# First attention of a two-layer transformer block: its prologue in another order

## The reference

```python
x = x + tanh(g_xattn[0]) * L0_xattn(layernorm(x), ctx, ctx, Wq, bq, Wk, bk, Wv, bv, Wo, bo)   # 16 heads of 16
x = x + tanh(g_ffn[0])   * L0_ffn(layernorm(x), ...)        # slot routing, top 8 of 64
x = x + tanh(g_xattn[1]) * L1_xattn(ctx, layernorm(x), ...) # 8 heads of 128
x = x + tanh(g_ffn[1])   * L1_ffn(layernorm(x), ...)        # quantized gated FFN

def L0_xattn(Q, K, V, ...):
    q, k, v = Q @ Wq + bq, K @ Wk + bk, V @ Wv + bv
    scores  = einsum('bhqd,bhkd->bhqk', q, k) / sqrt(16)
    return einsum('bhqk,bhkd->bhqd', softmax(scores), v) @ Wo + bo
```

## Time and profile before

| | us |
|---|---|
| three runs | 1004.11, 998.09, 996.44 |
| median | 998.09 |
| the profiled execution, its own time | 998.65 |
| its span in the profile | 996.9 |
| PE, DVE, ACT, POOL busy | 843.5, 720.1, 507.2, 73.2 |

### The profile page before, as it was taken

One profiled execution on the slowest core, in us unless ns is written; L12 is line 12 of the kernel. 1 busy time (PEld: TensorE's weight loads), 2 busy tenths in 40 slices (PEclk: granted clock), 3 DMA queues, 4 the chain that ended last, 5 costly groups with the idle time before them and its releaser, 6 DMA issues. The chain is left out here.

```text
span 996.9 us, 16711 instructions
## 1 busy us (share of the span) xinstructions
PE 843.5 (85%) x5560; PEld 675.4 (68%) x5563; DVE 720.1 (72%) x1646; ACT 507.2 (51%) x1056; POOL 73.2 (7%) x135
## 2 busy tenths in 40 slices
PE   3359999996557659999999989999899999995657
PEld 3247777764334547888888868888688888884223
DVE  6337788774558548888888768788688887775777
ACT  2036666663314125655556546556455565553665
POOL 1000101000130000000000000000000000000241
PEclk9669999999768769999999989999999999998797
DMA  3362222201300040000000000000000000000002
GB/s 103 106 195 81 85 85 85 75 19 30 152 0 1 1 116 12 2 0 12 1 11 2 1 14 2 1 12 1 4 12 1 1 1 1 1 1 18 13 0 85
DMA packets 37518, 33.41 MB, mean 34 GB/s; under 512 B 9586, under 2 KB 36276, under 8 KB 37172
## 3 DMA queue, kind: packets, MB, share of 16 engines
q1 hardware_dynamic: 37428, 32.28, 10.1%
...
## 5 line engine op out<-in xcount | busy, mean ns | idle before, releaser
L1367 ACT ACTIVATE c_probs<-c_pS,c_neg_max 128x512 f32<-128x512 f32 x128 | 88.2, 689 | 120.2 <-DVE c_neg_max L1489 120.1
L1489 DVE TENSOR_REDUCE c_neg_max<-c_pS 128x1 f32<-128x512 f32 x128 | 88.3, 690 | 70.6 <-PE c_pS L1690 68.8
L454 DVE TENSOR_REDUCE a_neg_max<-a_pS 128x2 f32<-128x512 f32 x128 | 82.4, 687 | 17.5 <-PE a_pS L621 17.0
L322 ACT ACTIVATE a_probsT<-a_pT 128x512 f32<-128x512 f32 x128 | 69.6, 597 | 48.3 <-PE a_pT L637 47.3
L1484 DVE TENSOR_TENSOR c_pT_lo<-c_pT,c_pT_hi 128x512 fp32r<-128x512 f32 x128 | 87.1, 681 | 1.3 <-ACT c_pT_hi L1375 1.3
L1707 PE MATMUL c_pO<-c_pT_hi,c_v_hi 128*128 128x256 f32 x256 | 77.4, 302 | 3.1 <-DVE c_pT_lo L1484 3.1
L1697 PE MATMUL c_pT<-ident,c_probs 128*128 128x128 f32 x512 | 77.5, 274 | 0.3 <-DVE c_probs L1496 0.3
L1697 PEld LDWEIGHTS c_pT<-ident,c_probs 128*128 128x128 f32 x512 | 64.3, 142 | 18.2 <-DVE c_probs L1496 0.7
L1380 ACT ACTIVATE c_oT<-c_pO,c_bv 128x256 f32<-128x256 f32 x64 | 30.4, 475 | 85.9 <-PE c_pO L1707 83.2
L1375 ACT CAST c_pT_hi<-c_pT 128x512 fp32r<-128x512 f32 x128 | 74.0, 579 | 0.0
L1707 PE MATMUL c_pO<-c_pT_hi,c_v_lo 128*128 128x256 f32 x256 | 72.0, 281 | 0.0
...
## 6 DMA issues: line engine op xcount, KB each, us to landing
...
a_ctx_in<-in_ctx_dram SPq DMA_DIRECT2D x8, 256.0 KB, 2.8
...
ctx_in<-in_ctx_dram SPq DMA_DIRECT2D x8, 256.0 KB, 2.7
out_dram<-x_sb SPq DMA_DIRECT2D x8, 256.0 KB, 2.2
x_sb<-in_x_dram SPq DMA_DIRECT2D x1, 1280.0 KB, 6.5
...
```

The source lines that it names most:

```text
L322: nc.scalar.activation(probsT[:, r // 2 % 2, 2 * (r % 2) + e, :, :], pT[:, e, :, :], ACT.Exp).then_inc(s["exp"], 1)
L454: nc.vector.tensor_reduce(neg_max[:, r // 2 % 2, :, e, r % 2], pS[:, e, :, :], AX_X, ALU.max, negate=True).then_inc(s["max"], 1)
L1367: nc.scalar.activation(probs[:, u % 4, :], pS[:, u % 2, :], ACT.Exp, bias=neg_max[:, u % 4:u % 4 + 1], accum_out=sums[:, u % 4:u % 4 + 1]) ...
L1489: nc.vector.tensor_reduce(neg_max[:, u % 4:u % 4 + 1], pS[:, u % 2, :], AX_X, ALU.max, negate=True).then_inc(s["max"], 1)
```

## The change

- **SP**: x 0 is loaded ahead of Wk, context 1 and x 1 ahead of the gates, x 2 ahead of batch 0's stacks, and `bo`, `wo` ahead of the rest of x. Batch 0's stacks get a function of their own (`first_stacks`): within K and Q the transfers that read high parts come first, those of K start at `k_hi` and no longer at `k_lo`, and SP issues 18 of the 24.
- **ACT** issues the other six (Q, first half). It also makes the high parts of Wk, Wq and Wv, the scaling of Wq and the bias column `bkq`, all of which DVE did.
- **DVE** keeps the low parts, in four instructions of 128 columns for each of Wk and Wq where there were eight of 64. Its prologue order is new, and the first four maxima stand between the low parts of batch 1.
- **POOL** takes the memsets of `one`, `max_parts` and `v_ones` and the bias rows (four instructions on one partition), which stand ahead of the first reciprocal root `rstd_of(0)`.
- **PE** does the bias matmuls and K's projection ahead of `xnT(0)`, V's projection ahead of `xnT(1)`, and interleaves the first scores with the projections of batch 1.
- The two waits for `load_o` ahead of `in_order` are gone. One stands in `out_project`, one in `out_bias`, both only for a batch number 0 that is known when the program is written.

```diff
--- before.py
+++ after.py
...
+        K_ROWS = ((0, 0), (2, 0), (1, 1))
+        Q_ROWS = ((0, 0), (1, 0), (2, 1))
+
+        def place(eng, parts, stack, which, half, par):
+
+            for i, part in which:
+                for e in range(HP):
+                    eng.dma_start(stack[64 * e + DK * i:64 * e + DK * i + DK, par, 4 * half:4 * half + 4, :].bitcast(F32),
+                                  parts[64 * e:64 * e + 64, part, half * T:(half + 1) * T].bitcast(F32)).then_inc(s[("stack0", "stack1")[half]], DMA)
...
-                    place(k_parts, k_stack, (0, 1, 0), half, par)
+                    place(sp, k_parts, k_stack, K_ROWS, half, par)
                     if half == 0:
                         pause(sp, s["q_lo"], n + 1, s["sp_passed"])
-                    place(q_parts, q_stack, (0, 0, 1), half, par)
+                    place(sp, q_parts, q_stack, Q_ROWS, half, par)
+
+            def first_stacks():
+
+                sp.wait_ge(s["k_hi"], 1)
+                place(sp, k_parts, k_stack, K_ROWS[:2], 0, 0)
+                sp.wait_ge(s["k_lo"], 1)
+                place(sp, k_parts, k_stack, K_ROWS[2:], 0, 0)
+                place(sp, k_parts, k_stack, K_ROWS, 1, 0)
+                sp.wait_ge(s["q_lo"], 1)
+                place(sp, q_parts, q_stack, Q_ROWS, 1, 0)
...
             load_ctx(0)
+            sp.dma_start(x_sb[:, 0:TT, :], x_view[:, 0:TT, :]).then_inc(s["x0"], DMA)
             sp.dma_start(w_raw[:, 1, :, :], a["L0_xattn_Wk"].rearrange("(c p) n -> p c n", p=P)).then_inc(s["load_k"], DMA)
-            sp.dma_start(x_sb[:, 0:TT, :], x_view[:, 0:TT, :]).then_inc(s["x0"], DMA)
...
+            load_ctx(1)
+            sp.dma_start(x_sb[:, TT:2 * TT, :], x_view[:, TT:2 * TT, :]).then_inc(s["x1"], DMA)
             sp.dma_start(gates[:, 0:2], a["g_xattn"].partition_broadcast(P)).then_inc(s["load_g"], DMA)
             sp.dma_start(gates[:, 2:4], a["g_ffn"].partition_broadcast(P)).then_inc(s["load_g"], DMA)
-            load_ctx(1)
-            sp.dma_start(x_sb[:, TT:2 * TT, :], x_view[:, TT:2 * TT, :]).then_inc(s["x1"], DMA)
-            stacks(0, 0, False)
+            sp.dma_start(x_sb[:, 2 * TT:3 * TT, :], x_view[:, 2 * TT:3 * TT, :]).then_inc(s["x2"], DMA)
+            first_stacks()
             load_ctx(2)
-            sp.dma_start(x_sb[:, 2 * TT:3 * TT, :], x_view[:, 2 * TT:3 * TT, :]).then_inc(s["x2"], DMA)
             stacks(1, 1, False)
-            sp.dma_start(x_sb[:, 3 * TT:NT, :], x_view[:, 3 * TT:NT, :]).then_inc(s["x"], DMA)
             sp.dma_start(bo[:, :], a["L0_xattn_bo"].partition_broadcast(P)).then_inc(s["load_o"], DMA)
             sp.dma_start(wo[:, :, :], a["L0_xattn_Wo"].rearrange("(c p) n -> p c n", p=P)).then_inc(s["load_o"], DMA)
+            sp.dma_start(x_sb[:, 3 * TT:NT, :], x_view[:, 3 * TT:NT, :]).then_inc(s["x"], DMA)
...
+            pool.memset(one[:, :], 1.0).then_inc(s["brow"], 1)
+            pool.memset(max_parts[:, :, :, :].bitcast(F32), 0.0).then_inc(s["zeros"], 1)
+            pool.memset(v_ones[:, :, :, :, DK:VW], 1.0).then_inc(s["ones"], 1)
...
+            pool.wait_ge(s["load_b"], 2 * DMA)
+            for i, factor in enumerate((1.0, DK ** -0.5)):
+                for j in range(DC):
+                    last = nc.gpsimd.tensor_scalar(bias_row[0:1, i, :].rearrange("p (j e d r) -> p j e d r", j=DC, e=HP, d=DK)[:, j, :, :, :],
+                                                   bias_raw[0:1, i, :].rearrange("p (j r e d) -> p j e d r", j=DC, e=HP, d=DK)[:, j, :, :, :], factor, None, ALU.mult)
+            last.then_inc(s["brow"], 1)
             rstd_of(0)
-            rstd_of(1)
-
...
+            rstd_of(1)
...
+            def weights_hi(i, done):
+                for c, j in COLUMNS:
+                    last = nc.scalar.copy(by_place(w_hi[:, i, :, :])[:, c, j, :, :, :], by_head(w_raw[:, i, :, :])[:, c, j, :, :, :])
+                last.then_inc(s[done], 1)
...
             ctxT_hi(0, 0, pV)
-            xnT_hi(0, pP)
+            act.wait_ge(s["load_k"], DMA)
+            weights_hi(1, "wk")
+            act.wait_ge(s["load_q"], DMA)
+            nc.scalar.mul(w_raw[:, 0, :, :], w_raw[:, 0, :, :], DK ** -0.5).then_inc(s["scale"], 1)
+            act.wait_ge(s["scale"], 1)
+            weights_hi(0, "wq")
+            act.wait_ge(s["bias_ps"], 1)
+            nc.scalar.copy(bkq[:, :, :].rearrange("p i j -> p (i j)"), pS[:, 0, 0, 0:2 * DC]).then_inc(s["bias"], 1)
             act.wait_ge(s["bias"], 1)
             k_high(0, pK)
+            xnT_hi(0, pP)
+            act.wait_ge(s["load_v"], 2 * DMA)
+            nc.scalar.copy(w_hi[:, 2, :, :], w_raw[:, 2, :, :]).then_inc(s["wv"], 1)
             q_high(0, pV)
+            act.wait_ge(s["q_hi"], 1)
+            place(act, q_parts, q_stack, Q_ROWS[:2], 0, 0)
             ctxT_hi(1, 1, pK)
+            act.wait_ge(s["q_lo"], 1)
+            place(act, q_parts, q_stack, Q_ROWS[2:], 0, 0)
+            xnT_hi(1, pV)
             act.wait_ge(s["load_g"], 2 * DMA)
             nc.scalar.activation(gates[:, :], gates[:, :], ACT.Tanh).then_inc(s["gate"], 1)
-            xnT_hi(1, pV)
             k_high(1, pP)
             q_high(1, pK)
             shift_out(0, 0)
...
+            def weights_lo(i, done):
+
                 dve.wait_ge(s[done], 1)
-                for c, j, e in COLUMNS:
-                    last = nc.vector.tensor_tensor(by_place(w_lo[:, i, :, :])[:, c, j, e, :, :], by_head(w_raw[:, i, :, :])[:, c, j, e, :, :],
-                                                   by_place(w_hi[:, i, :, :])[:, c, j, e, :, :].bitcast(F32), ALU.subtract)
+                for c, j in COLUMNS:
+                    last = nc.vector.tensor_tensor(by_place(w_lo[:, i, :, :])[:, c, j, :, :, :], by_head(w_raw[:, i, :, :])[:, c, j, :, :, :],
+                                                   by_place(w_hi[:, i, :, :])[:, c, j, :, :, :].bitcast(F32), ALU.subtract)
...
+                if isinstance(m, int) and m == 0:
+                    dve.wait_ge(s["load_o"], 2 * DMA)
...
-            dve.memset(max_parts[:, :, :, :].bitcast(F32), 0.0).then_inc(s["zeros"], 1)
+            ctxT_lo(0, 0, pV)
             norm_stats(0)
             norm_moments(0)
-            dve.wait_ge(s["load_k"], DMA)
-            weights(1, "wk")
-            ctxT_lo(0, 0, pV)
+            weights_lo(1, "wk")
             norm_apply(0)
-
-            dve.wait_ge(s["load_b"], 2 * DMA)
...
-            dve.wait_ge(s["load_q"], DMA)
-            nc.vector.tensor_scalar(w_raw[:, 0, :, :], w_raw[:, 0, :, :], DK ** -0.5, None, ALU.mult).then_inc(s["scale"], 1)
+            weights_lo(0, "wq")
+            k_low(0, pK)
             xnT_lo(0, pP)
-            dve.wait_ge(s["scale"], 1)
-            weights(0, "wq")
-            dve.wait_ge(s["bias_ps"], 1)
-            nc.vector.tensor_copy(bkq[:, :, :].rearrange("p i j -> p (i j)"), pS[:, 0, 0, 0:2 * DC]).then_inc(s["bias"], 1)
-            k_low(0, pK)
-            q_low(0, pV)
+            dve.wait_ge(s["wv"], 1)
+            nc.vector.tensor_tensor(w_lo[:, 2, :, :], w_raw[:, 2, :, :], w_hi[:, 2, :, :].bitcast(F32), ALU.subtract).then_inc(s["wv"], 1)
             norm_stats(1)
             norm_moments(1)
-            dve.wait_ge(s["load_v"], 2 * DMA)
-            nc.vector.tensor_copy(w_hi[:, 2, :, :], w_raw[:, 2, :, :]).then_inc(s["wv"], 1)
-            dve.wait_ge(s["wv"], 1)
-            nc.vector.tensor_tensor(w_lo[:, 2, :, :], w_raw[:, 2, :, :], w_hi[:, 2, :, :].bitcast(F32), ALU.subtract).then_inc(s["wv"], 1)
+            q_low(0, pV)
             norm_apply(1)
             ctxT_lo(1, 1, pK)
-            dve.memset(v_ones[:, :, :, :, DK:VW], 1.0).then_inc(s["ones"], 1)
+            dve.wait_ge(s["ones"], 1)
+            v_out(0, 0, pO[:, :, :].rearrange("p a t -> p (a t)"))
             xnT_lo(1, pV)
-            v_out(0, 0, pO[:, :, :].rearrange("p a t -> p (a t)"))
+            pair_max(0, 0, 0)
             k_low(1, pP)
+            pair_max(1, 0, 1)
             q_low(1, pK)
-            for r in range(4):
-                pair_max(r, r // 2, r)
-            dve.wait_ge(s["load_o"], 2 * DMA)
+            pair_max(2, 1, 2)
+            pair_max(3, 1, 3)
             dve.wait_ge(s["gate"], 1)
             in_order(dve, batch)
             out_bias(B - 2)
...
                 pe.wait_ge(s["onT_sb"], m + 1)
+                if isinstance(m, int) and m == 0:
+                    pe.wait_ge(s["load_o"], 2 * DMA)
...
             pe.wait_ge(s["ident"], 1)
             ctxT(0, pV, (s["ident"], 1))
-            xnT(0, pP, (s["ident"], 1))
-            pe.wait_ge(s["wk"], 2)
-            project_k(0, 0, pK, (s["ident"], 1))
-            pe.wait_ge(s["brow"], 3)
+            pe.wait_ge(s["brow"], 2)
             for i in range(2):
                 for j in range(DC):
                     last = nc.tensor.matmul(pS[:, 0, 0, DC * i + j:DC * i + j + 1], bias_row[0:1, i, j * P:(j + 1) * P], one[:, :], start=True, stop=True)
             last.then_inc(s["bias_ps"], 1)
```

(14 more changed lines are left out.)

25 lines of the change are left out of this document (3 added, 22 removed).

## The result

| | median us | lowest to highest | runs |
|---|---|---|---|
| before | 1000.02 | 996.44 to 1004.11 | 4 |
| changed | 984.02 | 982.55 to 987.53 | 4 |

The ratio is 0.985, 95% interval 0.982 to 0.9879: the change makes the kernel 1.2 to 1.8% faster. In medians that is 16.0 us (14.1 against the 998.09 that the prediction started from, before the fourth run), where 23.6 were forecast; the forecast of 974.5 was 9.5 too low, and 984.02 lies just outside the range of 970 to 983. The profiled execution took 984.09, its span 982.3.

The account below looks back on a forecast made before the run. A prologue of latencies, chiefly the wait for `wo`, then PE-bound batches: batch 0 starts 26.5 earlier, context 3 and batch 2's stacks cut the gain to 23.6; 998.65 - 23.6 = 975.0, as median 974.5 us, range 970 to 983.

Parts of the forecast that it names:

- Removed wait: PE's wait for the output weights ahead of batch 0 goes: 15.8 us of that batch's earlier start.
- K of batch 0: Prologue chain from Wk's load through bias matmuls and projection to K's high part: about 13.0, where it was 17.2.
- the prediction's second rule: DVE and POOL exclude each other on SBUF: up to 1 us added to K's chain, total 975.5.
- Stacks of batch 0: SP's 18 and ACT's six stack transfers: ACT's issues out at 22.0, landed 23.9; SP's landed at 26.1.
- T: SP's issue of the load behind batch 1's stacks: claimed to move from 53.5 to 44.2.
- Start of batch 0: PE takes up batch 0 at 35.5 instead of 62.04, 26.5 earlier: 15.8 removed wait, 10.7 new order.
- What is given back: PE's wait for context 3 cuts the gain to 24.6, ACT's wait for batch 2's stacks to 23.6 us.
- Batch 2's stacks: SP's 24 stack issues behind the loads take 15.3 to 17.6; with 16 they are landed at 71.1.
- rival 4: Slower than before: batch 2's stack issues behind the big loads take up to 1.835 us each; 1002.5, chance 0.03.
- rival 2: Prologue slower than summed, by issues on two queues or late bias rows: T 5 later, gain 18.6, 979.5; chance 0.22.
- rival 3: Only the wait comes out, K's chain no shorter and T unmoved: gain 14.5, 983.6; chance 0.08.
- the four signs of being wrong: First K issue after 15, ACT's six issues above 3.8, stack issues above 0.7 each, new waits after 80 us.

Follow-up runs that it names:

- e1_wait_only: Kernel before, with only the two waits for the output weights moved as in the change: 987.92 us, ratio 0.9891.
- e6_bias_behind: Changed kernel with FFN loads behind the last batch's stacks, and PE's bias matmuls behind K's projection: 976.78 us, one execution.
- e7_bias_dve: Changed kernel with FFN loads behind the last stacks, PE's bias matmuls behind K's projection, bias rows on DVE instead of POOL: 978.09 us, ratio 0.9775.
- e3_wait_next_late: Kernel before, with the two output-weight waits moved and the FFN loads behind the last stacks, without the new prologue: 981.93 us, ratio 0.9839.
- e9_k_held: Changed kernel with FFN loads behind the last stacks, SP issuing K's second half only after Q's low part: 975.43 us, ratio 0.9754.
- e12_change_again: The changed kernel run and profiled again without further edits: 983.61 us, ratio 0.9829 to the kernel before.
- e2_next_late: Changed kernel with the six FFN weight loads issued behind the last batch's stacks: 976.46 us, ratio 0.9778 to the kernel before.

## Why the prediction was wrong, step by step

**Removed wait: right.** No wait for `wo` is left; `e1_wait_only` prices it alone at 15.1 at batch 0's start (15.8 forecast).

**K of batch 0: 2.5 too early.** First K issue 15.47 against 13.0. POOL's four bias instructions took 2.68, 0.66 each, where I took 0.3 from rows of other work with an upper bound of 0.40: the bound itself failed. The bias matmuls (four in the program, eight in the rows) took 1.86 where they had taken 1.05. That they now come behind a pause of PE is not the reason, or not the only one: behind a projection they took 1.86 too in `e1_wait_only`, `e6_bias_behind` and `e7_bias_dve`, and 1.05 in `e3_wait_next_late`. The casts on ACT took 1.34 and DVE's low part 1.29, where I had 1.0 twice. `e7_bias_dve` shows that most of POOL's share can be taken out without an effect, since PE's work behind Wk's low part comes next. The 1 us that the prediction's second rule would add did not come: Wk's low part took 1.29 beside POOL's bias rows and 1.21 in `e7_bias_dve`, where they are not on POOL.

**Stacks of batch 0: 3.9 too early.** ACT's six issues began at 19.67 against 17.7 and were out at 23.59 against 22.0; the issues themselves took 0.64 each, against 0.62. Then 4.2 for the landing where 1.9 was taken, a price of one queue. (Q's projection took 1.7 where I had 2.3 as a mean of full and half clock; the rows that I read as half clock have a granted clock of 1.00.) The Trainium skill (DMA: Bandwidth & Descriptors, Issuing engines are not separate DMA queues) had warned that a second issuing engine saves only sequencer time. By it T would have been 2.7 later. The runs agree with it in part: without ACT's share T was 51.83 and 51.96, with it 50.80 in the execution that compares (48.22 in the one with the faster Q projection), so 1.0 to 1.2 were saved, and the total moved by no more than the intervals hide. Meanwhile the DMA engines were busy for 93% of the time against 26.8%, and the median landings were 3.6 to 4.2 against 2.6; that the transfers slowed each other is the likely reason, which `e9_k_held` supports. The truth lay between the rule and my row.

**T: 49.25 against 44.2**, the sum of the above: 3.9 at the scores, 0.5 at batch 1's K, 0.6 in the stacks. **Start of batch 0: 38.37 against 35.5**, fewer than T's five since maxima, scores and projection overlap more closely than summed (and the sum's own terms, 33.7 and 1.6, make 35.3).

**What is given back is the step that failed: the distances from T.** I had taken them from the kernel before as fixed: SP free of the loads at T + 8.4, so batch 2's stacks from T + 8.9, and context 3 landed at T + 16.0. In the change SP was free at T + 10.7, the stacks began at T + 12.4, and context 3 came at T + 18.95. With T five late (49.25 against 44.2) the stacks were 5.0 + 3.5 = 8.5 late and context 3 8.0, of the 8.6 us missing at ACT's high part of K for batch 3. The stacks ended last: ACT waited 0.48 for them, so by this trace an earlier context 3 alone would have brought half a microsecond at most (in the repeat, `e12_change_again`, context 3 ended last, at T + 20.4). Taking the FFN loads out of the queue (`e2_next_late`) freed both.

The queue of loads was named as what to watch. What I did not do was ask how firm T and the distances were, though the gain hung on them one for one from the moment that PE no longer slept; a T late by t costs t at the end, while the start of batch 0 itself, on which most of the working was spent, had 5.5 us to spare. Nor did I read that in the kernel before SP had waited 2.7 us for PE ahead of context 3 and had issued nothing behind it for ten. The order of the loads was changed too (`bo` and `wo` ahead of x), and I costed that at nothing; what it cost is open.

**Batch 2's stacks: their own price right.** From the first issue, 61.65, to the landing took 18.1 where the sum had 18.0. Stack issues behind the loads took 0.63 each (3.76 for six), so rival 4, 1.835 each and slower than before, found nothing: the backlog sits in the loads' own issues and in what lands behind them.

**Behind: right.** Batches of 22.1 and no new waits; 1.5 of the profiled execution's span went at the last projection, in a stretch with a granted clock of 0.82.

**The rivals.** What happened is rival 2 (T 5 later, gain 18.6) with another 3.5 from the longer distance to batch 2's stacks. Its 5 came out by luck: the late bias rows were in it, but the issues of ACT and SP did not take each other's time, the landings grew instead. Its chance of 0.22 was too small against 0.50 for a forecast that needed several prices that no row showed to hold together; bias rows, casts and landing all cost more than I took, Q's projection alone less. Its price was also cut short, T + 5 with unchanged distances. The range ended at 983 and should have reached the near half of rival 3. Two of the four signs of being wrong did show: K's first stack issue later than 15 (15.47), and ACT's six issues above 3.8 together (3.86, barely).
